# New slot tables for the shared PSUM bank, and VectorE's units of four steps shifted by one step

## What is computed

```
x  = x + attention(layernorm(x)) ; x = x + ffn(layernorm(x))
q, k, v = split_heads(x @ Wq.T), ... ; q, k, v = exp_map(q, c), exp_map(k, c), exp_map(v, c)
arg  = max(1 + 2c * |q-k|^2 / max((1 - c|q|^2)(1 - c|k|^2), EPS), 1 + EPS)
w    = softmax(-beta * arccosh(arg) / sqrt(c) - bias)        # 8 x 16 x 1024 x 1024
out  = log_map(exp_map(w @ log_map(v))) @ Wo.T
ffn  = dequant(to_fp8(x / s_in) @ to_fp8(kernel / s_k)) + bias
```

## Time and profile before

| | us |
|---|---|
| median of 3 runs | 1992.56 |
| lowest, highest | 1990.39, 1993.75 |
| the profiled execution's own time | 1994.49 |
| its span in the trace | 1992.7 |

### The profile page before, as it was taken

How to read it: one execution, slowest core, us unless ns; L and a number is a source line. 1 busy time by engine, 2 the same in 40 slices (tenths; PEclk the granted TensorE clock), 3 DMA queues, 4 the chain that set the end, 5 groups by cost and what they waited for, 6 DMA issues and landing times.

```text
span 1992.7 us, 29554 instructions
## 1 busy us (share of the span) xinstructions
PE 1788.6 (90%) x10713; PEld 603.1 (30%) x10713; DVE 1142.9 (57%) x2825; ACT 1869.9 (94%) x1094; POOL 12.8 (1%) x35
## 2 busy tenths in 40 slices
PE   7988989989898798989998898998989899899897
PEld 4322222323232232322322223232322223233234
DVE  7454565655656656565656647565565656323436
ACT  4889999999999799999998999999999999999883
POOL 2000000000000000000000000000000000000000
PEclk9799999999999899999999899999999999999889
DMA  1314213141312213132040321314131131411110
GB/s 56 112 49 144 54 54 103 42 134 43 112 44 78 77 44 112 43 101 75 23 134 22 110 67 44 112 43 134 40 107 52 56 90 43 123 43 53 33 33 23
DMA packets 112953, 142.54 MB, mean 72 GB/s; under 512 B 35691, under 2 KB 61548, under 8 KB 112748
## 3 DMA queue, kind: packets, MB, share of 16 engines
q1 hardware_dynamic: 112748, 140.13, 22.6%
HBM read 85.07 MB, written 55.05 MB: 70 GB/s over the span
## 4 chain that ended last, share of the span: by engine, by line
ACT 54%; PE 24%; issue 14%; DVE 4%; ACTq 3%; DMA 0%; DVEq 0%; SPq 0%
ACT U L1217 28%; ACT U L1224 26%; PE ps L1100 8%; PE ps L401 6%; PE ps L1115 5%; ACTq L1265 2%; PE ps L695 2%; DVE U L1294 1%; PE ps L1138 1%; PE ps L406 1%; PE ps L1142 1%; DVE U L1285 1%; DVE rows L554 0%; DMA U<-in_L_attn_W_o_dram 0%; ACT e L529 0%
## 5 line engine op out<-in xcount | busy, mean ns | idle before, releaser
L1224 ACT ACTIVATE U<-U 128x2048 f32<-128x2048 f32 x512 | 997.1, 1949 | 0.3
L1217 ACT ACTIVATE U<-ps 128x2048 f32<-128x2048 f32 x500 | 955.7, 1911 | 35.5 <-PE ps L1100 31.6
L1100 PE MATMUL ps<-q_T,k_T 18*128 18x512 f32 x4096 | 632.5, 652 | 133.0 <-ACT U L1217 107.7
L1115 PE MATMUL ps<-U,vals 128*32 128x512 f32 x4096 | 560.4, 620 | 29.4 <-ACT U L1224 28.9
L1100 PEld LDWEIGHTS ps<-q_T,k_T 18*128 18x128 f32 x4096 | 195.9, 187 | 356.8 <-ACT U L1217 296.4
L401 PE MATMUL ps<-wT,xnT 128*128 128x384 f32 x512 | 232.0, 545 | 4.9 <-DVEq L1318 2.5
L490 DVE COPY qkv<-ps 128x384 f32<-128x384 f32 x112 | 62.4, 557 | 243.7 <-PE ps L401 243.6
L1115 PEld LDWEIGHTS ps<-U,vals 128*32 128x32 f32 x4096 | 81.7, 109 | 205.4 <-ACT U L1224 159.2
L401 PEld LDWEIGHTS ps<-wT,xnT 128*128 128x128 f32 x512 | 81.1, 194 | 197.0 <-issue 132.4
L1138 PE MATMUL ps<-woT,ident 128*128 128x256 f32 x340 | 121.8, 441 | 3.8 <-DVEq L1318 3.6
L406 PE MATMUL ps<-ident,rows 128*128 128x128 f32 x512 | 107.2, 308 | 4.9 <-DVE rows L554 2.4
(11 more groups left out here) (209 smaller groups left out, 1179.6 us busy)
## 6 DMA issues: line engine op xcount, KB each, us to landing
...
```

What stands on the lines that cost most here:

```text
L1100: ins = pe.matmul(g.ps[:, 2 * pair + i, :], a.k_T[HB * h:HB * h + RD, b % 2, hg, kt * P:(kt + 1) * P], a.q_T[HB * h:HB * h + RD, G % 3, hg ...
L1115: ins = pe.matmul(g.ps[HB * h:HB * h + VW, 6, :], a.vals[:, b % 2, kt, (hg * HPG + h) // 2, DH * (h % 2):DH * (h % 2) + VW], U[:, n % RING ...
L1217: act.activation(U[:, n % RING].rearrange("p b n -> p (b n)"), chunk(n), ACT.Ln, scale=-2.0 / EPS, bias=1.0).then_inc(freed, 1)
L1224: act.activation(U[:, n % RING], U[:, n % RING], ACT.Exp, scale=exponent).then_inc(exp_done, 1)
```

## The change

Four things are rewritten. First, the slots of the uses: both X stand in slot 4, M0 in 5, M1 in 7, M2 in 8 and so on, A0 behind S in slot 30 and A1 in slot 34 behind Q0's second part; R2 and R5, which had shared their steps with A0 and A1, get both halves of theirs. BARE becomes three steps: 5, 8 and 16. Second, the pieces: squares one step earlier in part, one Newton step each in 17, 18 and 19, nrm in 19 as before, ScalarE's e from slot 21 to 20, the writing of vals from slot 20 to 35 (31 for projection 2), the first row scaling of a projection from piece 24 into 23 (with the sides in the other order); in the finish 8, 28 and 32 become 7, 27 and 33, its store moves by one slot and the projection's by two. Third, VectorE's unit: it does bound and clamp of n and then copies and pieces of n-1, so it starts one step earlier against the copies. Fourth, in an open unit the pieces listed in PROJECT_LATER and FINISH_LATER wait until the unit's last clamp has been issued. Block 15 has its own short table of finish slots.

```diff
-PROJECT_USES = {("X", 0): (4, BOTH), ("X", 1): (5, BOTH),
-                ("M", 0): (7, BOTH), ("M", 1): (8, BOTH), ("M", 2): (9, BOTH), ("M", 3): (10, BOTH),
-                ("M", 4): (12, BOTH), ("M", 5): (13, BOTH), ("M", 6): (15, BOTH), ("M", 7): (16, BOTH),
-                ("R", 0): (25, BOTH), ("R", 1): (26, BOTH), ("R", 2): (27, 0), ("A", 0): (27, 1),
-                ("R", 3): (28, BOTH), ("R", 4): (29, BOTH), ("R", 5): (31, 0), ("A", 1): (31, 1),
-                ("R", 6): (32, BOTH), ("R", 7): (33, BOTH)}
+PROJECT_USES = {("X", 0): (4, 0), ("X", 1): (4, 1),
+                ("M", 0): (5, BOTH), ("M", 1): (7, BOTH), ("M", 2): (8, BOTH), ("M", 3): (10, BOTH),
+                ("M", 4): (11, BOTH), ("M", 5): (13, BOTH), ("M", 6): (15, BOTH), ("M", 7): (16, BOTH),
+                ("R", 0): (25, BOTH), ("R", 1): (26, BOTH), ("R", 2): (27, BOTH), ("R", 3): (28, BOTH),
+                ("R", 4): (29, BOTH), ("A", 0): (30, 1), ("R", 5): (31, BOTH), ("R", 6): (32, BOTH),
+                ("R", 7): (33, BOTH), ("A", 1): (34, 1)}
...
-BARE = 7
-SHORT_SLOTS = {23: (23, 24), 24: (25, 26), 25: (27, 28), 26: (29,), 27: (30, 31), 28: (32,), 29: (33,), 30: (), 31: ()}
+BARE = (5, 8, 16)
+SHORT_SLOTS = {18: (18, 21), 19: (19, 22), 20: (20, 23), 21: (24,), 22: (25,), 23: (26,), 24: (27,), 25: (28,),
+               26: (29,), 27: (30, 31, 32), 28: (33,), 29: (34,), 30: (), 31: ()}
+
+PROJECT_LATER = (0, 1, 2, 9, 12, 13, 16, 17, 18, 21, 22, 24)
+FINISH_LATER = (3, 4, 6, 21, 22, 23, 24, 25, 26, 27, 33)
...
-        if k == 21:
+        if k == 20:
             act.wait_ge(n_rdy, n + 1)
             act.activation(e[:, :, :], nrm[:, :, :], ACT.Exp, scale=g.M2SC).then_inc(e_rdy, 1)
...
-        if k in (9, 11, 14, 17):
-            t = {9: 0, 11: 1, 14: 2, 17: 3}[k]
+        if k in (9, 12, 13, 16):
+            t = {9: 0, 12: 1, 13: 2, 16: 3}[k]
...
-        if k == 18:
+        if k == 17:
             root_guess(v, step, ss[:, :, :], y[:, :, :])
             newton(v, step, ss[:, :, :], y[:, :, :], y2[:, :, :], 1)
+        if k == 18:
+            newton(v, step, ss[:, :, :], y[:, :, :], y2[:, :, :], 1)
         if k == 19:
-            newton(v, step, ss[:, :, :], y[:, :, :], y2[:, :, :], 2)
+            newton(v, step, ss[:, :, :], y[:, :, :], y2[:, :, :], 1)
             v.tensor_tensor(nrm[:, :, :], ssqk, yqk, ALU.mult).then_inc(n_rdy, 1)
-        if k == 20:
+        if k == (31 if n == 2 else 35):
...
+                def pieces(n, which):
+
+                    G, s = n // STEPS, n % STEPS
+                    for m, k in finished(G, s):
+                        if (G < LAST and k in FINISH_LATER) in which:
+                            finish.vector(v, m, k)
+                    for m, k in projected(G, s):
+                        if (k in PROJECT_LATER and (m, k) != (2, 2)) in which:
+                            project.vector(v, m, k)
...
+                PROMPT, LATER, ALL = (False,), (True,), (False, True)
+
                 def unit(n0, is_open):
+
                     for n in range(n0, n0 + UNIT):
...
+                        if is_open:
+                            bound(n)
+                            clamp(n)
+                        if n:
+                            copies(n - 1)
+                            pieces(n - 1, PROMPT if is_open else ALL)
+                    if is_open:
+                        for n in range(max(n0, 1), n0 + UNIT):
+                            pieces(n - 1, LATER)
```

More of the change, by code:

```diff
@@ L538, in first_vector @@
         step(v.tensor_scalar(ss[:, :, :], ss[:, :, :], EPS * EPS, None, ALU.max))
-        vector(v, n, 18, step)
-        vector(v, n, 19, step)
-        if n == 0:
-            v.wait_ge(zeroed, ZEROED)
-        vector(v, n, 20, step)
+        for k in (17, 18, 19, 35):
+            if k == 35 and n == 0:
+                v.wait_ge(zeroed, ZEROED)
+            vector(v, n, k, step)
         vector(v, n, 21, step)
@@ L629, in vector @@
             v.tensor_reduce(amax[:, :], a4[:, :, :].rearrange("p t h -> p h t"), AX.X, ALU.max).then_inc(amax_rdy, 1)
+            if n >= 2:
+                scale_rows(v, n, (0,))
         if k == 24:
-            scale_rows(v, n, (1, 0))
-        assert first or step.n == OWN.get(k, 0), (k, step.n)
+            scale_rows(v, n, (1,))
+        assert first or k in (31, 35) or step.n == OWN.get(k, 0), (k, step.n)
     p = Shared()
@@ L670, in sync @@
             if n >= 1:
-                sp.wait_ge(steps_v, PER * (n - 1) + sum(count for slot, count in OWN.items() if slot <= 28))
+                sp.wait_ge(steps_v, PER * (n - 1) + sum(count for slot, count in OWN.items() if slot <= 27))
             sp.dma_start(xt[:, :, :], g.x_g[n]).then_inc(f_in, 16)
-        if k == 33:
+        if k == 34:
             sp.wait_ge(res_rdy, n + 1)
@@ L1172, in _ @@
                         use(*key, 0)
-                    unused = n > 2 and s != BARE and not in_step(G, s, 0) + in_step(G, s, 1)
+                    unused = n > 2 and s not in BARE and not in_step(G, s, 0) + in_step(G, s, 1)
                     if unused:
@@ L1326, in copy, with copies @@
                         project.copy(v, n, (kind, i))
+                def copies(n):
+                    G, s = n // STEPS, n % STEPS
+                    for key in in_step(G, s, 0):
+                        copy(*key)
+                    for key in in_step(G, s, 1):
+                        copy(*key)
+                    if n % KT == 0 and n >= KT:
+                        copy_sums(n // KT - 1)
+                def pieces(n, which):
+                    G, s = n // STEPS, n % STEPS
+                    for m, k in finished(G, s):
[4 more added lines that the diff above has]
+                            project.vector(v, m, k)
+                    if G == LAST and False in which:
+                        finish.last_early(v, s)
+                    if n == QUERY_STEP and False in which:
+                        project.scale_rows(v, 1, (0,))
+                    if n == KERNEL_STEP and False in which:
+                        setup.vector_kernel(v)
@@ L1328, in unit @@
+                PROMPT, LATER, ALL = (False,), (True,), (False, True)
                 def unit(n0, is_open):
                     for n in range(n0, n0 + UNIT):
-                        G, s = n // STEPS, n % STEPS
-                        if is_open and n + 1 < n0 + UNIT:
-                            bound(n + 1)
-                            clamp(n + 1)
-                        for key in in_step(G, s, 0):
-                            copy(*key)
-                        for key in in_step(G, s, 1):
-                            copy(*key)
@@ L1366, in _ @@
                         v.wait_ge(rqb_in, 16 * (n0 // KT + 1))
-                        bound(n0)
-                        clamp(n0)
                         unit(n0, True)
@@ L1384, in general_flag @@
                     v.tensor_copy(g.flag[:, :], g.ps[0:1, 0, 0:1]).then_inc(max_steps, 1)
+                copies(N - 1)
+                pieces(N - 1, ALL)
                 copy_sums(NG * HG - 1)
```

52 lines of the change are left out of this document (21 added, 31 removed).

## The result

| | before | after |
|---|---|---|
| median, us | 1991.5 | 2043.6 |
| lowest, highest | 1984.8, 1993.9 | 2036.1, 2051.2 |
| runs | 6 | 6 |
| profiled execution's span | 1992.7 | 2034.3 |

The ratio is 1.027, with a 95% interval of 1.024 to 1.030: the change costs about 52 us, where 16 were forecast. The profiled execution of the changed kernel is the fastest of its six; the others lie up to 15 us above, at a lower mean granted clock (0.957 to 0.965 against its 0.967). So the trace shows 41.6 us of span more, and some 10 us of the difference of the medians lie in executions without a trace.

A forecast was written before the change was run, and what follows sets the result against it. ScalarE, busy 94%, bounds the kernel, so only its waits count. Middle blocks +36.6, open units -10 and first and last blocks -10.8 give +15.8 on 1992.6: 2008 us, 8-in-10 range 1978 to 2018.

The forecast's parts named there:

- third rival: Bare steps lower the clock wherever finish and projection leave them empty, and junctions cost 2.5 us each: 2020 to 2027, chance 0.05.
- M apart: Middle blocks: a gap after each pair of M products lets TensorE catch up, -0.38 us a block, -5 us.
- e early: At s = 16 and 17, e waits 1.2 us for nrm: net +1.0 us a block, 13 blocks, +13 us.
- junction: From s = 30 to s = 6 of the next block, delays of 1.9 us each, +24 us in all.
- block 5, open unit: Pieces between block 5's clamps go behind the last clamp or away, 2 us comes back: -8 us (-12 to -5).
- block 8, open unit: Block 8: row scaling stays ahead of the bound, postponed pieces delay R2's copy: -2 us (-4 to 0).
- blocks 0 and 15: First and last blocks: -5.4 us for block 0 and -5.4 for block 15, together -10.8 us.
- (a): Junction: A1 waits for Q0's copy and delays the distances, so the next log is 0.35 us late.
- (b): Junction: A1's chain and normalising x on VectorE delay Y0's copy; ScalarE loses another 0.6 to 0.85 us.
- (c): Junction, s = 0: vals between the copies of Y and X0 delays X1 and the distances, +0.4 to +0.8 us.
- (d): Junction: M0 in s = 1 and normalising S behind the adds of finish piece 33 give 0.2 to 0.5 us more.
- The first and second rival: First: junction delay absorbed, 1984 us, chance 0.20. Second: no middle-block stall real, 1967 us, chance 0.10.

The follow-up runs named there:

- run 1: The changed kernel with only ScalarE's e back in slot 21: 2005.4 us, ratio 1.006.
- run 11: The changed kernel with e back in slot 21 and the writing of vals back in slot 20: 2008.4 us, ratio 1.008.
- run 3: The changed kernel with e back in slot 21 and no bare steps (BARE empty): 2018.5 us, ratio 1.014.
- run 7: The changed kernel with A1 back in slot 31 and e back in slot 21, A0 left in slot 30: 1974.0 us, ratio 0.992.
- run 9: The changed kernel with A1 back in slot 31, e back in slot 21 and both lists of postponed pieces empty: 1976.4 us, ratio 0.993.
- run 10: The changed kernel with VectorE's old unit order, A0 and A1 back in slots 27 and 31, e in slot 21: 1980.1 us, ratio 0.995.
- run 4: The changed kernel with A0 and A1 back in slots 27 and 31, R2 and R5 in first halves alone: 2017.9 us, ratio 1.014.
- run 6: The changed kernel with VectorE's unit order as before and nothing postponed, so the tables alone: 2039.2 us, ratio 1.026.
- run 2: The changed kernel with BARE empty, so steps 5, 8 and 16 have idle-filling products again: 2031.8 us, ratio 1.021.
- run 5: The kernel before with only VectorE's shifted unit and the postponed pieces of open units: 1997.2 us, ratio 1.004.
- run 8: The kernel before with only the changed table of projection 2 and the short finish table of block 15: 1982.0 us, ratio 0.996.

## Why the prediction was wrong

The sign was right and the stalls that I named were there; the size was off by a factor of three, 52 us against 16, beyond every case that I had, the third rival's 2027 too. By the terms, from before's profiled execution to after's (41.6 us of span; the measured column adds up to 43, with roundings and small stretches left out):

| term | forecast | measured |
|---|---|---|
| M apart | -5 | +0.5; -3.3 once A1 is back |
| e early | +13 | +14.5 (12.5 in the 12 blocks, 1.0 each in 5 and 8) |
| A0 behind S | +4.6 | +3.2 |
| junction | +24 | +22.7, and 3.4 in blocks 5 and 8 |
| log of s = 19 | none | +13.9, and 1.8 each in blocks 5 and 8 |
| block 5, open unit and what follows it | -8 | -1.7: -7.9 in s = 3 to 9, +6.2 in s = 10 to 16 |
| block 8, open unit | -2 | +2.8 |
| blocks 0 and 15 | -10.8 | -17.8, and 2 ahead of the first log (not there in runs 1 and 11) |

**The step that failed** is the clock. I had the drop as a property of bare steps in block 15 and as a third rival, at 0.05, and gave a stall of ScalarE in a middle block its own length as its price. The term that is missing, the late log of s = 19, is 17.5 of the 26 us by which the profiled execution exceeds the forecast; that the other executions of the changed kernel have still lower clocks and longer times points the same way, but no trace of them shows where.

In the runs the stall's price is itself plus what TensorE's idle time does to the clock: 1.3 us of stall at s = 17 brought 1.6 to 2.5 us more at s = 19 in 8 of 13 blocks, and the junction's 1.2 to 1.7 us became 2.4 to 2.9 where the clock fell behind it. Runs 1, 3, 7, 9, 10 and 11, without e's stall, have no late log at s = 19; with the stall and the bare step, run 4 has 10 of 13 and run 6 has 12; run 2, with the stall but the step filled, has 3. So the stall is needed at this place, and the bare step makes the drop likelier. The third rival looked for the drop at each empty step; in the middle blocks it came at an empty step behind a stalled one. In block 15 an empty step was followed by a drop without any stall in the kernel before and in runs 1 and 9, and by none in run 5. The Trainium skill (TensorE: Matmul & The Clock Gate, section "HAM oscillation — how this bites in real kernels") has the clock fall when a wait for a DMA leaves TensorE idle, and the next work start cold. Here the trace agrees that idle time stands ahead of the drop (2.28 us, a wait for ScalarE and not for a DMA), but in block 3 the distances right behind it still ran at the full clock (1.24 us), and only the products after them at half.

**Junction.** The sum was right by luck, as its parts were not. (a) and (b), A1 behind Q0 and its chain ahead of Y0's copy, were put at 0.95 and measured 1.0 a block (run 6: 0.7 to 1.3), but not where I had them: (a) was to make the first log behind it 0.35 us late, and that log is on time. The load of `opens` ahead of Y0's copy, 0.3 to 0.7, was not in it, though the order shows it in front of the copies of each fourth step. (c) and (d), vals, both X in one step and M0, were put at 0.95 (with 0.55 for (d), which is above its own range of 0.2 to 0.5), and are next to nothing: run 4 has them all and is at 0.0, run 11 takes vals out for 2 us in all. (No run takes both X or M0 out while A1 stands in its new slot.) The logs of s = 31 and 0 kept their 3.55 us, and a junction has two late logs, s = 1 and 2, where I had three to five. What filled their place is the clock (six middle blocks with a drop at s = 1, 1.1 us each).

**M apart** was right in kind, 5.5 to 2.2 us in runs 4 and 7, a gain of 3.3 where 5 were forecast. In the changed kernel the junction's lag reaches into s = 3 to 6 and takes it back.

**Open units.** Block 5's -8 came out at -1.7. The gain in the unit itself, put at 10, is 7.9, and that the postponed pieces bring "2 us" back is the term that was mis-sized: 6.2 us, 5.6 of them in one log, since 7.5 us of pieces and 1.6 us of the load stand ahead of one copy, and the clock falls there too. In block 8 there was a loss of 2.8 instead of a small gain. In runs 1 and 2 the same unit takes 12.0 and 12.1 us, below before's 12.8, with the clock at half for 13.6 us in and just ahead of it, where the changed kernel has 23.9 and the kernel before 17.0; so the loss varies with the clock, and its cause stays open.

**Ends.** Blocks 0 and 15 gave 7 us more than put down, and part of it is chance. Block 0's share was 9.1 us here and 3 in runs 1 and 10, which have the same tables for it (its -5.4 in the forecast doesn't follow from the terms beside it: -5.9 + 1.7 + 0.2 + 1.1 is -2.9). In block 15 the short table takes the forecast 4.3 us away (run 8), and the 4 us of the old bare step are gone too; but run 5, which keeps the old table and that step, is without 3.4 and 3.9 of them as well. The +3.7 for new bare steps did not come in the profiled execution, but in runs 1 and 9 the logs of s = 3 to 9 of block 15 are 4.0 us late with a clock drop there.

**The first and second rival**, 0.30 together, had the stalls absorbed. Nothing absorbed them: of e's 1.19 us of wait, 1.0 a block came out in the logs.
